# A seventh PSUM bank in the ring of a three-block attention kernel, with its order of steps shifted

## What is computed

```python
x = x + block0(x, cond_256, cond_64)   # x @ input_basis.T * c1 @ mtr * c2 @ output_basis, rank 64
# block 1: attention and SwiGLU, each behind an RMS norm with gain and bias from cond_256
x = x + attention(rmsnorm(x, t), Wq, Wk, Wv, Wo)      # 16 heads of 16 features
x = x + (silu(y @ gate_w.T) * (y @ hid_w.T)) @ out_w.T # y = rmsnorm(x, t), hidden 1024
# block 2: attention with q, k, v biases, weighted by a coherence per position and head
attn = softmax(q @ k.T / 4)
mod = attn * coh / (sum(attn * coh) + 1e-8)
mod = 0.79 * mod + 0.21 * field_attention             # the same row of 256 for all heads
x = x + (mod @ v) @ Wout.T + bout
# block 3: masked attention, RMS norm of its result, scale and shift from cond_256
out = (softmax(where(mask, -inf, q @ k.T / 4)) @ v) @ Wo.T
x = x + out / rms(out) * rms_scale * (1 + sc) + shift
```

## Time and profile before

| what | value |
|---|---|
| time, median of 3 runs | 1535.89 us (1534.87 to 1536.75) |
| time of the profiled execution | 1535.91 us |
| its span in the profile | 1534.1 us |
| PE busy | 1446.8 us, 94% |
| DVE busy | 1097.2 us, 72% |
| ACT busy | 705.6 us, 46% |
| POOL busy | 269.0 us, 18% |

### The profile page before, as it was taken

One profiled execution on the slowest core, in us unless ns is written; L12 is line 12 of the kernel. 1 busy time (PEld: TensorE's weight loads), 2 busy tenths in 40 slices (PEclk: granted clock), 3 DMA queues, 4 the chain that ended last, 5 costly groups with the idle time before them and its releaser, 6 DMA issues. The chain is left out here.

```text
span 1534.1 us, 29407 instructions
## 1 busy us (share of the span) xinstructions
PE 1446.8 (94%) x10234; PEld 1204.5 (79%) x10282; DVE 1097.2 (72%) x3686; ACT 705.6 (46%) x1539; POOL 269.0 (18%) x323
## 2 busy tenths in 40 slices
PE   2669999999999999999999999999999999999996
PEld 1457888888888888888888787787877887887874
DVE  7757666666666666665656867768678889889884
ACT  1325434343444444433335555555555555555553
POOL 7401000000000000000013232232320111111112
PEclk9879999999999999999999999999999999999998
DMA  7065222332322333232224545445355455445450
GB/s 282 1 86 81 47 40 50 50 50 43 49 42 38 50 50 50 33 63 33 43 43 78 82 57 75 67 61 84 55 75 83 74 77 97 75 76 97 74 77 22
DMA packets 101116, 100.00 MB, mean 65 GB/s; under 512 B 11478, under 2 KB 97624, under 8 KB 100330
## 3 DMA queue, kind: packets, MB, share of 16 engines
q1 hardware_dynamic: 100970, 98.14, 38.1%
HBM read 16.83 MB, written 4.19 MB: 14 GB/s over the span
## 5 line engine op out<-in xcount | busy, mean ns | idle before, releaser
L963 ACT ACTIVATE work<-bank 128x512 f32<-128x512 f32 x768 | 448.6, 598 | 275.9 <-PE bank L1149 223.9
L1149 PE MATMUL bank<-qs,ks 98*128 98x256 f32 x1536 | 410.1, 350 | 0.5 <-DMA qs<-nm 0.5
L528 DVE TENSOR_REDUCE rowmax<-bank 128x2 f32<-128x512 f32 x512 | 337.7, 679 | 100.6 <-PE bank L1139 99.9
L1139 PE MATMUL bank<-ks,qs 96*128 96x256 f32 x1536 | 337.6, 302 | 21.4 <-DMA ks<-qk_lo 10.0
L1149 PEld LDWEIGHTS bank<-qs,ks 98*128 98x128 f32 x1536 | 277.3, 192 | 37.3 <-issue 6.0
L1139 PEld LDWEIGHTS bank<-ks,qs 96*128 96x128 f32 x1536 | 243.2, 191 | 45.1 <-DMA ks<-qk_lo 16.9
L525 DVE CUSTOM_DVE_ANT_0 c1t<-bank,big_q 128x256 bf16<-128x256 f32 x512 | 190.3, 420 | 0.4
L1161 PE MATMUL bank<-work,vp 128*32 128x256 f32 x3072 | 185.7, 382 | 0.0
L989 ACT ACTIVATE work<-bank 128x256 f32<-128x256 f32 x128 | 49.0, 383 | 235.3 <-PE bank L1198 235.3
L583 DVE SCALAR_TENSOR_TENSOR work<-work,bank 128x256 f32<-128x256 f32 x128 | 53.4, 418 | 128.8 <-ACT work L989 127.7
L1161 PEld LDWEIGHTS bank<-work,vp 128*32 128x32 f32 x3072 | 90.0, 109 | 62.4 <-ACT work L963 0.2
(11 more groups left out here) (209 smaller groups left out, 1813.5 us busy)
## 6 DMA issues: line engine op xcount, KB each, us to landing
qs<-qk_hi SPq DMA_DIRECT2D x192, 128.0 KB, 3.9
ks<-qk_hi SPq DMA_DIRECT2D x192, 128.0 KB, 3.8
qs<-qk_lo SPq DMA_DIRECT2D x96, 128.0 KB, 4.4
ks<-qk_lo SPq DMA_DIRECT2D x96, 128.0 KB, 4.3
xres<-in_x_t SPq DMA_DIRECT2D x4, 1024.0 KB, 9.0
x_in<-in_x SPq DMA_DIRECT2D x16, 256.0 KB, 2.8
out<-xres SPq DMA_DIRECT2D x16, 256.0 KB, 2.1
qs<-nm SPq DMA_DIRECT2D x96, 16.0 KB
```

What stands on the lines that cost most here:

```text
L528: a = dve.tensor_reduce(rowmax[:, :, k:k + 1], bank[:, :].rearrange("p (t s) -> p t s", t=TC), AX, ALU.max)
L963: act.activation(probs[:, place[n, b, k], :, :], bank[:, :].rearrange("p (c s) -> p c s", c=TC), ACT.Exp, scale=HD ** -0.5)\
L1139: m = pe.matmul(bank[:, t * S:(t + 1) * S], qs[par][0:SCORE_ROWS, k, t * P:(t + 1) * P], ks[par][0:SCORE_ROWS, k, :], start=True, stop=True)
L1149: m = pe.matmul(bank[:, c * S:(c + 1) * S], ks[par][0:SHIFTED_ROWS, k, c * P:(c + 1) * P], qs[par][0:SHIFTED_ROWS, k, :], start=(n != 3), ...
```

## The change

The ring gets the seventh bank. A pair of pv steps now takes one use of it, like any other step, at the place in the order where the first of the two stands. The use is given back when DVE has transposed the bank. The next pair no longer waits for that transpose by name; it waits for the reader of whatever had its bank seven uses earlier. So does every other user of the ring.

Besides, the table shifts. The diff, cut to its core:

```diff
     1: {
-        "max": (-6.11, 4.35), "xT": -26.99, ... "squares": -30.51, ... "wo": 21.54,
-        "down": (27.4, 1.24)
+        "max": (-6.11, 4.35), "xT": -26.32, ... "squares": -28.61, ... "wo": 21.71,
+        "down": (27.4, 1.18)
     2: {
-        "stack": (-23.72, -22.05, -15.9, -15.63), "coh3": -10.31
+        "stack": (-23.72, -21.22, -15.9, -15.63), "coh3": -10.7
     3: {
-        "norm": (10.2, 15.99), "neg": (-6.23, 1.31), "k": -21.53, "mod": 14.15, "oT": 16.94, "wo": 20.71
+        "norm": (10.2, 15.39), "neg": (-6.26, 2.22), "k": -23.17, "mod": 14.36, "oT": 17.22, "wo": 20.21
...
-        pv_bank, acc_bank = banks[6], banks[7]
+        acc_bank = banks[7]
...
-        head = middle = back = Ring(sem("banks_full"), banks[0:6])
+        head = middle = back = Ring(sem("banks_full"), banks[0:7])
...
+                if what == "pv":
+                    return [(head, f"pv{k // 2}", self.o_raw, k // 2 + 1)] if k % 2 == 0 else []
...
-                        if k % 2 == 0 and not (n == 1 and b == 0 and k == 0):
-                            pe.wait_ge(L.o_raw.sem, L.o_raw.at(b, k // 2))
+                        bank = head.bank(n, b, f"pv{k // 2}")
+                        if k % 2 == 0:
+                            head.wait_free(pe, n, b, f"pv{k // 2}")
...
+                                if k % 2 and c == TC - 1 and i == HG - 2:
+                                    m.then_inc(head.sem, 1)
```

More of the change, by code:

```diff
@@ L42 @@
         "smax": -13.9, "pv": (8.3, 16.3), "rz": (8.59, 16.41), "norm": (8.44, 16.81), "neg": (-6.41, 1.59),
-        "max": (-6.11, 4.35), "xT": -26.99, "q": -24.35, "stack": (-25.3, -22.08, -15.9, -16.88), "k": -22.83, "v": -12.2,
-        "load": -46, "rank": -32.95, "cond": -30.74, "squares": -30.51, "xn": -28.27, "oT": 18.5, "wo": 21.54, "yn": 23.31,
-        "yT": 24.38, "ffn": (25.73, 1.15), "down": (27.4, 1.24)},
+        "max": (-6.11, 4.35), "xT": -26.32, "q": -24.35, "stack": (-25.3, -22.08, -15.9, -16.88), "k": -22.83, "v": -12.2,
@@ L46 @@
+        "load": -46, "rank": -32.95, "cond": -30.74, "squares": -28.61, "xn": -28.27, "oT": 18.5, "wo": 21.71, "yn": 23.31,
+        "yT": 24.38, "ffn": (25.73, 1.15), "down": (27.4, 1.18)},
     2: {
         "smax": -14.72, "pv": (9.43, 17.26), "rz": (9.93, 17.56), "norm": (14.07, 17.86), "neg": (-6.46, 1.15),
-        "max": (-6.52, 2.71), "xT": -26.47, "q": -24.49, "stack": (-23.72, -22.05, -15.9, -15.63), "k": -24.09, "v": -11.32,
-        "load": -30, "coh1": -13.18, "coh2": -10.81, "coh3": -10.31, "vsum": 1.0, "sumv": 4.0, "field": 5.0, "oT": 19.5,
+        "max": (-6.52, 2.71), "xT": -26.47, "q": -24.49, "stack": (-23.72, -21.22, -15.9, -15.63), "k": -24.09, "v": -11.32,
@@ L50 @@
+        "load": -30, "coh1": -13.18, "coh2": -10.81, "coh3": -10.7, "vsum": 1.0, "sumv": 4.0, "field": 5.0, "oT": 19.5,
         "wo": 22.05},
     3: {
-        "smax": -13.86, "pv": (9.2, 15.39), "rz": (9.7, 15.69), "norm": (10.2, 15.99), "neg": (-6.23, 1.31),
-        "max": (-6.13, 2.38), "xT": -26.55, "q": -24.57, "stack": (-24.46, -20.12, -15.9, -15.03), "k": -21.53, "v": -13.4,
-        "mod": 14.15, "oT": 16.94, "wo": 20.71, "squares": 23.07, "resid": 24.6},
+        "smax": -13.86, "pv": (9.2, 15.39), "rz": (9.7, 15.69), "norm": (10.2, 15.39), "neg": (-6.26, 2.22),
@@ L55 @@
+        "max": (-6.13, 2.38), "xT": -26.55, "q": -24.57, "stack": (-24.46, -20.12, -15.9, -15.03), "k": -23.17, "v": -13.4,
+        "mod": 14.36, "oT": 17.22, "wo": 20.21, "squares": 23.07, "resid": 24.6},
 }
-LATER = {"vector": {"q": -0.2, "k": 0.5, "ffn": 0.3, "oT": 0.5, "field": -0.34, "pv": 0.6, "coh2": 0.46, "squares": 0.41, "rz": 0.8, "norm": 1.2, "v": -0.29, "xn": 0.23, "stack": 1.16, "xT": -0.21}, "scalar": {"wo": 1.0, "pv": 0.2, "yn": -0.02, "oT": -0.25, "xn": -0.04, "ffn": -0.24, "xT": -0.33}, "gpsimd": {"max": -0.28, "oT": -0.14, "q": -0.42, "xn": -0.41}, "sync": {"k": -0.01}}
+LATER = {"vector": {"q": -0.2, "k": 0.5, "ffn": 0.3, "oT": 0.5, "field": -0.34, "pv": 0.6, "coh2": 0.46, "squares": 0.41, "rz": 0.8, "norm": 1.2, "v": -0.29, "xn": 0.23, "stack": 1.16}, "scalar": {"wo": 1.0, "pv": 0.2, "yn": -0.02, "oT": -0.25, "xn": -0.04, "ffn": -0.24, "xT": -0.33}, "gpsimd": {"max": -0.5, "oT": -0.14, "q": -0.42, "xn": -0.41}, "sync": {"k": -0.01}}
@@ L544, in step @@
                         dve.wait_ge(L.pv.sem, L.pv.at(b, k + 1))
-                        dve.transpose(ot_raw[:, DC * u:DC * (u + 1), :].rearrange("p c s -> p (c s)"), pv_bank[:, :]).then_inc(L.o_raw.sem, 1)
+                        dve.transpose(ot_raw[:, DC * u:DC * (u + 1), :].rearrange("p c s -> p (c s)"), head.bank(n, b, f"pv{u}")[:, :]).then_inc(L.o_raw.sem, 1)
                     if what == "rz":
@@ L1160, in step @@
                                 j = HG * k + i
-                                m = pe.matmul(pv_bank[HW * i:HW * (i + 1), (k % 2) * S:(k % 2 + 1) * S], vp[par][:, c, DC * (j % HALF) + j // HALF, :],
+                                m = pe.matmul(bank[HW * i:HW * (i + 1), (k % 2) * S:(k % 2 + 1) * S], vp[par][:, c, DC * (j % HALF) + j // HALF, :],
                                               probs[:, place[n, b, j], c, :], start=(c == 0), stop=(c == TC - 1))
+                                if k % 2 and c == TC - 1 and i == HG - 2:
+                                    m.then_inc(head.sem, 1)
                         m.then_inc(L.pv.sem, 1)
```

## The result

The kernel after takes 1543.04 us (median of 5 runs, 1542.18 to 1543.44), the kernel before on the same chip 1536.56 (5 runs, 1534.87 to 1538.51). The ratio is 1.004, with a 95% interval of 1.0027 to 1.0053: the change makes the kernel slower by 0.4%, 6.5 us. The forecast said +2.9 us and placed it just inside of "no change". Its range ended at 1543.0, 7.1 us above its starting point; the measured time is 0.04 us past that end, the measured shift 0.6 us inside of it.

What follows compares the result with a forecast made beforehand. The prediction took TensorE, busy for 94% of the span, to bound the kernel. Beginning +0.6, layers 1 and 2 0, passage -0.5, layer 3 +5.2 and end -2.4 gave +2.9 us: 1538.8 us, range 1530.5 to 1543.0.

Steps and rivals of the forecast that it cites:

- Layer 3, +5.2: Steady batches of layer 3: k's earlier place makes VectorE late, so pv2 starts +0.40 us later, over 13 batches.
- the hold: Layer 3: neg0's first VectorE instruction waits until POOL's second add ends, finishing 1.4 us later than before.
- the two bounds: Layer 3 per batch: +0.40 us if neg0's first instruction is held by POOL's add, -0.21 if not.
- Layer 2, 0: Layer 2: PE's shorter waits for banks return as a longer wait for the ks transfer before smax0; 14 batches x 0.
- Rival 3: Layer 2: the transfers come earlier with the seven-bank ring, -4.9 to -12.6 us on top of +2.9; chance 8%.
- one late transfer: Layer 2: smax0 waits for ks<-qk_lo, whose arrival does not move, so PE waits 0.35 us longer for it.
- The passages, -0.5 forecast: Start of layer 3: some banks come free earlier, so smax0 waits less; -0.5 us, between 0 and -0.9.
- The beginning, +0.6: First batches: squares start 1.0 us later behind the exponential, less 0.4 from waits filled; between -1 and +3 us.
- the 0.4 us that I let the seventh bank give back: Beginning, 95 to 145 us: smax3 and the seventh bank may fill some 0.4 us of PE's waits.
- The end, -2.4: Last batches: with neg1 behind oT, wo starts 1.3 us earlier at full clock; probs8 then waits for the max transfer.
- "slower" at 0.38: Whole kernel: chance of a slower result, against 0.33 for same and 0.29 for faster.
- the first case: Whole kernel: the forecast itself, +2.9 us, with its own range 1536.0 to 1541.5; chance 45%.

Runs made afterwards that it cites:

- the two trials with SP's order: Seven banks, new table only in layer 3 except k; then layer 2's ks transfers, all three or high parts only, before the max transfer: 1551.35 and 1537.76 us.
- the run that failed here: Kernel after with layer 3's squares and resid steps earlier, which also moved resid's output transfer ahead of the qs transfers in SP's queue: 1545.42 us.

## Why the prediction went as it did

**Layer 3, +5.2: right in mechanism and size, with a part missing.** A steady batch lost 0.38 us against 0.40 forecast, by the hold, at the place and for the time worked out (0.98 us against some 0.95), and the two bounds came out as well: with no hold the period is 22.75, -0.24 against -0.21. The layer lost 6.0 us in all, because in two batches smax0 waited 0.39 and 0.45 us for the transfers into ks, and they became 0.64 and 0.69 us longer than the others. I had called neg0's later end harmless for them. But nm, and behind it in SP's queue the ks transfers, goes out 12.9 us behind a batch's wo in place of 12.2, while smax0 has moved by 0.4 only. That this alone makes the two batches is not shown: single longer batches occur with the ring alone too (one of 23.31 among those of 22.75), where nm is not late, and in the run with the adds early and SP's order kept the same two batches are 0.15 and 0.57 us longer with no hold at all.

**Layer 2, 0: right.** The waits moved from banks to the transfer, 0.52 us on average before smax0 against some 0.55 forecast, and the ring alone leaves the period as it is. Rival 3 is excluded by that run. The reason I gave, one late transfer, was too narrow: the two trials with SP's order show several that compete.

**The passages, -0.5 forecast, +1.6 measured: the step that failed.** Into layer 3 I took a gain of the banks, -0.5, and the ring alone shows none: 63.76 us, as before. I also left out that layer 3's table is at work there already, for its first batches while layer 2 ends. k's early place costs 0.8 us in this passage, and not by the hold, which hasn't begun; it stays at 64.63 us with the adds early and goes to 63.86 with k back. Into layer 2 I costed the down steps at nothing, "work that PE does anyway, in another order". That holds inside layer 1. At its end down7 stands ahead of the last v and puts it 0.86 us later, and behind v waits the load of the next layer's weights. I had looked for who waits for down, not for who waits for what down overtakes.

**The beginning, +0.6: the number right (+0.6), by luck as far as the runs show.** The loss at squares was 0.96 us as forecast. Over all fourteen profiled kernels the first wo comes at 139.7 to 142.4 us where squares stand early (mean of seven 141.0) and at 141.3 to 143.0 where they stand late (mean of seven 141.9). That points the way of the forecast, but kernels with the same order differ by more than the effect; the start of L495 alone varies by 1.9 us (75.5 to 77.4). No run shows the 0.4 us that I let the seventh bank give back.

**The end, -2.4: right (-2.6).** wo at full clock and earlier, then probs8 bound by the max transfer, are in the rows. That neg1's move alone brings all of it was wrong as far as seen: in both kernels that have it with six banks the end gained 1.2 us, and the clock fell behind smax11. The stretch behind the last wo was 0.5 us longer, which nobody forecast; the clock was at 0.75 there from 1530 to 1532 us. I don't put this down to the change, since the same stretch takes 10.3 to 12.0 us in kernels with the same order in it.

**The sum.** +2.9 became +6.3 in the profiled execution: 2.1 from the passages, 0.8 in layer 3, 0.5 behind the last wo, 0.2 in layer 2, less 0.2 at the end. With bounds on both sides of the 0.2% line, "slower" at 0.38 was the largest of the three chances, but the time named stood on the other side of the line. The range that I gave the first case, 1536.0 to 1541.5, doesn't follow from its bounds: with those of beginning, end and passage added it is 1536.8 to 1542.8.

## What to carry to other kernels

Before a step is moved on VectorE, look at what GpSimd does at the new time: a short SBUF instruction that starts beside a GpSimd operation may last as long as that operation, and the cost is the rest of it, not a share. A step of an order table stands on several engines; a trial that moves it moves its transfers too, as the run that failed here shows. And at the seams between stages ask who waits for each step that is overtaken: weights loaded over old ones wait for the last reader.

## What was not expected of the hardware

An instruction of VectorE that had never been long, L538 with its two SBUF inputs, was held for 1.26 us as soon as it started 0.05 us behind a GpSimd add; 0.2 us earlier L536 beside the end of the add before had passed in 0.17. A transfer of 16 KB took 2.4, 3.7 and 4.2 us from its issue to the product that waits for it, and in all but one of 27 cases this product started 0.1 to 0.7 us behind the landing of the last of the 128 KB transfers issued ahead. And the same wait of 1.5 us on TensorE was followed by a granted clock of 1.00 in one kernel and of 0.54 in another with the same order on PE.
